# First stage of a graph layer on one Trainium2 core: 16-bit sort masks by whole groups, ScalarE's pair work a group later, weights prepared later

## What is computed

```
hx   = einsum('ni,rio->rno', x, weight)          # one product per relation
msg  = hx[edge_type, src]                        # one row per edge
agg  = segment_sum(msg, dst, num_segments=50000)
node = agg * 0.5**0.5 + h_bias + (x @ loop_weight) * 0.5**0.5
out  = layernorm(x + node, eps=1e-5)             # per row, no scale or shift
```

## Time and profile before

| | us |
|---|---|
| median of 3 runs | 802.35 (802.19 to 805.64) |
| profiled execution, its own time | 802.23 |
| its span in the trace | 800.5 |
| busy PE / PEld | 674.3 / 597.8 |
| busy DVE / ACT / POOL | 575.1 / 477.2 / 417.0 |

### The profile page before, as it was taken

How to read it: one execution, slowest core, us unless ns; L and a number is a source line. 1 busy time by engine, 2 the same in 40 slices (tenths; PEclk the granted TensorE clock), 3 DMA queues, 4 the chain that set the end, 5 groups by cost and what they waited for, 6 DMA issues and landing times. The chain is left out here.

```text
span 800.5 us, 16173 instructions
## 1 busy us (share of the span) xinstructions
PE 674.3 (84%) x4648; PEld 597.8 (75%) x4648; DVE 575.1 (72%) x2146; ACT 477.2 (60%) x1143; POOL 417.0 (52%) x426
## 2 busy tenths in 40 slices
PE   1658777768999999999999999999999999999720
PEld 1436656757999999999899999877887788788510
DVE  7906899965565665665565678888898898898830
ACT  2546680255556665556655566778777777777721
POOL 1000000426777777777777630376676676776463
PEclk9969999889999999999999999999999999999955
DMA  5301000656777776778777678988899999998621
GB/s 170 123 16 48 1 0 1 190 196 212 229 236 260 251 237 240 223 232 280 240 240 222 201 244 287 287 297 301 292 326 333 322 317 323 305 325 302 226 87 45
DMA packets 78903, 173.44 MB, mean 217 GB/s; under 512 B 25744, under 2 KB 41426, under 8 KB 78817
## 3 DMA queue, kind: packets, MB, share of 16 engines
q1 hardware_dynamic: 59233, 125.16, 46.4%
q0 software_dynamic: 19584, 47.23, 18.0%
HBM read 100.47 MB, written 78.20 MB: 223 GB/s over the span
## 5 line engine op out<-in xcount | busy, mean ns | idle before, releaser
L727 DVE TENSOR_TENSOR xt_low<-xt_ps,xt_high 128x512 fp32r<-128x512 f32 x241 | 164.9, 685 | 130.0 <-ACT xt_high L938 129.7
L1116 PE MATMUL y_ps<-w_high,xt_high 128*128 128x256 f32 x752 | 213.9, 284 | 0.0
L1116 PE MATMUL y_ps<-w_low,xt_high 128*128 128x256 f32 x752 | 213.6, 284 | 0.0
L1116 PE MATMUL y_ps<-w_high,xt_low 128*128 128x256 f32 x752 | 213.4, 284 | 0.0
L520 POOL DMA_INDIRECT gathered<-in_x,src_at x105 | 108.6, 1034 | 175.0 <-DVE edge_at L721 143.3
L938 ACT ACTIVATE xt_high<-xt_ps 128x512 fp32r<-128x512 f32 x241 | 141.9, 589 | 72.9 <-PE xt_ps L1084 71.1
L973 ACT ACTIVATE y_out<-y_ps,rstd 128x256 f32<-128x256 f32 x376 | 156.3, 470 | 13.4 <-DMA out_rows<-y_out 12.9
L1116 PEld LDWEIGHTS y_ps<-w_high,xt_low 128*128 128x128 f32 x752 | 144.2, 192 | 8.3
L549 POOL DMA_INDIRECT out_rows<-y_fix,fix_at x99 | 98.4, 994 | 96.0 <-ACT y_fix L1012 73.0
L1116 PEld LDWEIGHTS y_ps<-w_low,xt_high 128*128 128x128 f32 x752 | 144.8, 193 | 0.2
L1116 PEld LDWEIGHTS y_ps<-w_high,xt_high 128*128 128x128 f32 x752 | 144.2, 192 | 0.0
(11 more groups left out here) (155 smaller groups left out, 992.8 us busy)
## 6 DMA issues: line engine op xcount, KB each, us to landing
x_in<-in_x SPq DMA_DIRECT2D x97, 512.0 KB, 4.8
out_rows<-y_out SPq DMA_DIRECT2D x97, 512.0 KB
message_in<-message_rows SPq DMA_DIRECT2D x99, 128.0 KB, 5.0
keys<-padded_dst SPq DMA_DIRECT2D x13, 508.0 KB, 7.3
w_rel<-in_L_gnn_weight SPq DMA_DIRECT2D x1, 2048.0 KB, 14.0
gathered<-in_x,src_at POOLq DMA_INDIRECT x105
message_rows<-message_out,edge_at POOLq DMA_INDIRECT x105
y_fix<-out_rows,fix_at POOLq DMA_INDIRECT x99
```

Source lines behind the costliest of these rows:

```text
L727: nc.vector.tensor_tensor(xt_low[:, q % XT_RING, :], xt_ps[q % 2][:, :], xt_high[:, q % XT_RING, :].bitcast(F32), ALU.subtract).then_inc(l ...
L1116: return nc.tensor.matmul(to, xt[:, at_row:at_row + P], w, start=start, stop=stop)
```

## The change

1. `startup` gets a new order and a parameter `late`. TensorE (`late` = 0) does pair k - 2 in step k, ScalarE (`late` = 1) its part of pair k - 3. Sorts follow a written-out pace: sort s comes in the first step k with 2.5 + 4 s < 4.9 (k - 3), ahead of the pair; what is left comes behind step 13. So step 4 has sort 0, step 5 sort 1, step 6 sorts 2 and 3, step 7 sort 4, and so on; sorts 12 and 13 are left for the end.
2. The sort masks of a group are made by three `tensor_tensor` instructions in 16 bit in place of 21 `tensor_scalar` in float32: an equality of tile numbers (7 x 106), an equality of lanes (7 x 128), and the product of the first with three fields (7 x 3 x 106), which waits for the first by a semaphore, `tiles_marked`. To fit 16 bit exactly, source and edge number are cut into three fields (`src_low`, the high bits of the source with the low bits of the edge, `edge_high`), and the lists are put together again from the 318 sums in eight steps.
3. TensorE's sort matmuls have 16-bit operands and 318 columns.
4. VectorE builds five groups of lane masks ahead in place of four, and the preparation of the weights (with two constants, `ones_r` and the zeroing of `bias_rows`) moves from ahead of the position chain to behind the masks of group 1 and the lane masks of group 6.
5. Behind the last group the lists come first, then offsets, then the relation weights. The wait for the last flag group moves behind `low(8)` and `low(9)`.
6. Counts: `total` is no longer copied out; one instruction adds and converts from PSUM.

```diff
+        FIELDS = 3
+        lane_of = keys[:, :, :, :].rearrange("p a b d -> p (a b d)")[:, 0:GROUP * P].bitcast(F16).rearrange("p (c l) -> p c l", l=P)
+        tile_of = sort_space[:, 0:2 * GROUP * FIELDS * MTP].rearrange("p (c v m) -> p c v m", v=FIELDS, m=MTP)
+        one_tile = sort_space[:, 2 * GROUP * FIELDS * MTP:2 * GROUP * (FIELDS + 1) * MTP].rearrange("p (c m) -> p c m", m=MTP)
-        flag_ps, sorted_ps, misc_ps = y_ps[3][:, 0:COLS + 2], y_ps[4][:, 0:2 * MTP], y_ps[5]
+        flag_ps, sorted_ps, misc_ps = y_ps[3][:, 0:COLS + 2], y_ps[4][:, 0:FIELDS * MTP], y_ps[5]
...
-        def startup(step_f, step_s, step_m):
-
-            m = 0
-            for k in range(GROUPS + 4):
-                if k < GROUPS:
-                    step_f(k)
-                if 1 <= k <= HOLD:
-                    step_m(k - 1)
-                if k >= 4:
-                    step_s(k - 4)
+        def startup(step_f, step_s, step_m, late):
+
+            sorts = 0
+            for k in range(GROUPS):
+                step_f(k)
+                while sorts < GROUPS and 2.5 + 4 * sorts < 4.9 * (k - 3):
+                    step_s(sorts)
+                    sorts += 1
+                if 0 <= k - late - 2 < HOLD:
+                    step_m(k - late - 2)
+            for k in range(sorts, GROUPS):
+                step_s(k)
...
-            for k in range(4):
+            for k in range(5):
                 build_lanes(k)
-
-            dve.wait_ge(loop_in, 16)
...
             dve.wait_ge(counts_summed, 1)
-            link(nc.vector.tensor_copy(total[:, :], misc_ps[:, R:2 * R]))
-            link(nc.vector.tensor_scalar(tot_f[:, :], total[:, :], float(P - 1), None, ALU.add))
-            link(nc.vector.tensor_copy(tot_i[:, :], tot_f[:, :]))
+            link(nc.vector.tensor_scalar(tot_i[:, :], misc_ps[:, R:2 * R], float(P - 1), None, ALU.add))
...
             def build_sort(k):
-                if k >= 2:
-                    dve.wait_ge(group_sorted, k - 1)
-                for c, slot in group_columns(k):
-                    nc.vector.tensor_scalar(lane_of[:, slot, :], iota_f[:, :], lo_f[:, c:c + 1], None, ALU.is_equal)
-                    nc.vector.tensor_scalar(tile_of[:, slot, 0, :], iota_f[:, 0:MTP], hi_f[:, c:c + 1], src_f[:, c:c + 1], ALU.is_equal, ALU.mult)
-                    last = nc.vector.tensor_scalar(tile_of[:, slot, 1, :], iota_f[:, 0:MTP], hi_f[:, c:c + 1], e1_f[:, c:c + 1], ALU.is_equal, ALU.mult)
-                last.then_inc(masks_sorted, 1)
+                cols = slice(k * GROUP, (k + 1) * GROUP)
+                to = slice((k % 2) * GROUP, (k % 2 + 1) * GROUP)
+                wait(dve, group_sorted, k - 1)
+                nc.vector.tensor_tensor(one_tile[:, to, :], lane_iota[:, 0:MTP].unsqueeze(1).broadcast_to([P, GROUP, MTP]),
+                                        tile_h[:, cols].unsqueeze(2).broadcast_to([P, GROUP, MTP]), ALU.is_equal).then_inc(tiles_marked, 1)
+                nc.vector.tensor_tensor(lane_of[:, to, :], lane_iota[:, :].unsqueeze(1).broadcast_to([P, GROUP, P]),
+                                        lane_h[:, cols].unsqueeze(2).broadcast_to([P, GROUP, P]), ALU.is_equal)
+                dve.wait_ge(tiles_marked, k + 1)
+                nc.vector.tensor_tensor(tile_of[:, to, :, :], one_tile[:, to, :].unsqueeze(2).broadcast_to([P, GROUP, FIELDS, MTP]),
+                                        fields[:, cols, :].unsqueeze(3).broadcast_to([P, GROUP, FIELDS, MTP]), ALU.mult).then_inc(masks_sorted, 1)
...
             for k in range(GROUPS):
                 build_sort(k)
-                if k + 4 < GROUPS:
-                    build_lanes(k + 4)
+                if k + 5 < GROUPS:
+                    build_lanes(k + 5)
+                if k == 1:
+                    prepare_weights()
...
+            dve.wait_ge(group_sorted, GROUPS)
+            link(nc.vector.tensor_copy(found[:, :], sorted_ps))
...
+            nc.vector.tensor_tensor(src_at[:, :], found_high[:, :], found[:, 0:MTP], ALU.add).then_inc(list_ready, 1)
+            link(nc.vector.tensor_tensor(found_edge[:, :], found_edge[:, :], found_low[:, :], ALU.add))
+            link(nc.vector.tensor_scalar(empty[:, :], found_edge[:, :], 0.0, float(SKIP), ALU.is_equal, ALU.mult))
+            nc.vector.tensor_tensor(edge_at[:, :], found_edge[:, :], empty[:, :], ALU.add).then_inc(list_ready, 1)
...
-            dve.wait_ge(flag_grouped, GROUPS)
             for part in range(8):
...
             low(HOLD)
             low(HOLD + 1)
+            dve.wait_ge(flag_grouped, GROUPS)
...
-            startup(flag_group, lambda k: None, raw_move)
+            startup(flag_group, lambda k: None, raw_move, 1)
...
-            startup(flag_group, sort_group, first_pair)
+            startup(flag_group, sort_group, first_pair, 0)
```

More of the change, by code:

```diff
@@ L211, in scratch @@
             return a if dt == F32 else a.bitcast(dt)
[L213 to L214 removed]
+        rel_i, src_i, dst_i, pos_i, hi_i, lo_i, e1_i, node_i, node_hi_i, src_high, edge_low, edge_high, src_low = (scratch(EC, I32) for _ in range(13))
+        rel_f, pos_f, e1_f, dead, node_lo, node_hi = (scratch(EC) for _ in range(6))
+        lane_h, tile_h = (scratch(EC // 2).bitcast(F16) for _ in range(2))
+        fields = scratch(FIELDS * EC // 2).bitcast(F16).rearrange("p (c v) -> p c v", v=FIELDS)
         onehot, running, placed = (scratch(R * EC) for _ in range(3))
@@ L226, in gnn_layernorm_kernel @@
         rel_n = scratch(MTP)
-        empty = scratch(MTP)
+        found = running[:, 0:FIELDS * MTP].bitcast(I32)
+        found_high, found_edge, found_low, empty = (running[:, (FIELDS + i) * MTP:(FIELDS + 1 + i) * MTP].bitcast(I32) for i in range(4))
         key_i, next_i = (onehot[:, i * P:(i + 1) * P].bitcast(I32) for i in range(2))
@@ L254, in gnn_layernorm_kernel @@
         masks_sorted = sem("masks_sorted")
+        tiles_marked = sem("tiles_marked")
         group_sorted = sem("group_sorted")
@@ L617, in _ @@
             nc.vector.tensor_copy(column_f[:, :], column_i[:, :])
[L618 to L622, removed]
+            nc.vector.tensor_copy(e1_f[:, :], e1_i[:, :])
+            nc.vector.tensor_scalar(edge_low[:, :], e1_i[:, :], 15, 6, ALU.bitwise_and, ALU.logical_shift_left)
+            link(nc.vector.tensor_scalar(edge_high[:, :], e1_i[:, :], 4, None, ALU.logical_shift_right))
+            nc.vector.tensor_copy(fields[:, :, 2], edge_high[:, :])
+            nc.vector.tensor_scalar(dead[:, :], e1_f[:, :], E + 0.5, 512.0, ALU.is_gt, ALU.mult)
             dve.wait_ge(rel_in, 32)
@@ L639, in _ @@
             dve.wait_ge(nodes_ready, 2)
+            link(nc.vector.tensor_tensor_scan(running[:, :], onehot[:, :], onehot[:, :], 0.0, ALU.add, ALU.max))
+            nc.vector.tensor_copy(prior[:, 1:R], rn[:, 0:R - 1, EC - 1])
+            dve.wait_ge(src_in, 32)
+            nc.vector.tensor_scalar(src_low[:, :], src_i[:, :], 1023, None, ALU.bitwise_and)
+            link(nc.vector.tensor_scalar(src_high[:, :], src_i[:, :], 10, None, ALU.logical_shift_right))
+            nc.vector.tensor_copy(fields[:, :, 0], src_low[:, :])
+            nc.vector.tensor_tensor(fields[:, :, 1], src_high[:, :], edge_low[:, :], ALU.add)
             def build_lanes(k):
@@ new lines, in prepare_weights @@
+            def prepare_weights():
+                dve.wait_ge(loop_in, 16)
+                dve.wait_ge(bias_in, 16)
+                link(nc.vector.tensor_scalar(w_main[:, :], w_main[:, :], C, None, ALU.mult))
+                for k in range(KT):
+                    d = w_main[:, k * D + k * P:k * D + k * P + P]
+                    link(nc.vector.tensor_tensor(d, d, ident[:, :], ALU.add))
+                wm = w_main[:, :].rearrange("p (k n) -> p k n", k=KT)
+                nc.vector.tensor_reduce(w_mean[:, 0:KT], wm, AX_X, ALU.add)
+                link(nc.vector.tensor_reduce(w_mean[:, KT:KT + 1], bias_b[:, :], AX_X, ALU.add))
+                link(nc.vector.tensor_scalar(w_mean[:, 0:KT + 1], w_mean[:, 0:KT + 1], 1.0 / D, None, ALU.mult))
+                for k in range(KT):
+                    d = w_main[:, k * D:(k + 1) * D]
+                    nc.vector.tensor_scalar(d, d, w_mean[:, k:k + 1], None, ALU.subtract)
+                nc.vector.tensor_copy(bias_rows[:, :], zero[:, :])
+                nc.vector.tensor_copy(ones_r[:, :], ones[:, :])
+                link(nc.vector.tensor_scalar(bias_b[:, :], bias_b[:, :], w_mean[:, KT:KT + 1], None, ALU.subtract))
+                nc.vector.tensor_copy(bias_rows[0:1, :].rearrange("p (t d) -> p t d", t=2), bias_b[0:1, :].unsqueeze(1).broadcast_to([1, 2, D]))
+                nc.vector.tensor_copy(bias_high[:, :], bias_b[:, :])
+                link(nc.vector.tensor_copy(w_high[:, :], w_main[:, :]))
+                nc.vector.tensor_tensor(bias_rows[32:33, :].rearrange("p (t d) -> p t d", t=2), bias_b[32:33, :].unsqueeze(1).broadcast_to([1, 2, D]),
```

(2 more changed lines are left out.)

44 lines of the change are left out of this document (10 added, 34 removed).

## The result

| | before | after |
|---|---|---|
| median, us | 803.12 of 4 runs (802.19 to 805.64) | 779.06 of 4 runs (778.44 to 779.61) |
| span of the profiled execution | 800.5 | 777.2 |
| first transpose of the main loop | 147.22 | 123.07 |
| from there to the end of the span | 653.3 | 654.1 |
| VectorE's stops ahead of sort masks | 31.5 in 5 | 11.4 in 1 |

The ratio is 0.9695, with a 95% interval of 0.967 to 0.972. The forecast was 777, within 769 to 785.

What follows compares the result with a forecast made beforehand. The first stage, paced by VectorE's sort masks and its 31.5 us of stops, was taken as the bound. It would end at 122.4 instead of 147.2; 800.5 - 24.8 + 1.7 = 777.4 us, range 769 to 785.

Steps and rivals of the forecast that it cites:

- Masks: VectorE's three 16-bit mask instructions: 4.25 us a group in place of 4.82, at 1.04 ns an element.
- The tail: From VectorE's last masks to the end of the first stage: 11.6 us, costing 3.3 against the kernel before.
- The stop: VectorE idle for 10.6 us, about 41 to 52, until sort 0 is done, as TensorE waits for the late weights.
- the first pair: TensorE's pair 0, from 41.2 once the weights are ready: 3.8 us up to ScalarE's move.
- The clock: TensorE's granted clock: low for four or five us from near 41, then 1.00 to about 86.
- (b): Rival: TensorE stays at the low clock through the pairs, step 7.9 us; 781 to 796 us, chance 0.07.
- (a): Rival: VectorE's 16-bit masks stream at twice the rate, group 3.4 us with lane masks; 755 us, chance 0.08.
- (c): Rival: the repeated 16-bit operand streams slower than f32 on VectorE; at double, about 834 us; chance 0.03.
- (d): Rival: VectorE's stop moves and its four later stops (7.9 us) come back; 785 us, chance 0.03.
- first gather: POOL's gathers start at about 115 in place of 147.44; counted as no gain, at most a microsecond.
- The part behind the stage: From the main loop's first transpose to the end: moves as a block, 653 us as now.
- is the sum of both engines' work: First stage, old order: a step adds TensorE's and ScalarE's work, 10.33 us at low clock, 8.02 at high.

Runs made afterwards that it cites:

- e4: The changed kernel with the weights prepared early, right behind the five groups of lane masks, ahead of the position chain: 767.65 us, ratio 0.956.
- e1: The changed kernel with the old order of startup, all else as changed: 819.1 us, ratio 1.021.
- e3: The kernel before with the new order of startup alone, f32 masks and early weights: 774.76 us, ratio 0.964.
- e7: e4 with the group's seven columns innermost in the masks, so TensorE reads at a step of seven elements: 784.77 us, ratio 0.977.
- e9: e5 with every lane, tile and field value stored twice side by side, masks still contiguous for TensorE: 748.27 us, ratio 0.932.
- e5: e4 with the offsets of the relations ahead of VectorE's wait for the last sort: 765.04 us, ratio 0.952.
- e10: e9 with the sorts a step earlier in the written order: 744.90 us, ratio 0.928.
- e2: e1 with the weights prepared early, where they were before the change: 805.67 us of 10 runs, ratio 1.0035.
- e8: e2 with fourteen useless matmuls ahead of each sort group on TensorE: 804.24 us of 12 runs, ratio 1.000.

## Why the prediction held

**Stage by stage.** Masks: 4.25 forecast, 4.24 measured. The masks of sort 0 started at 24.2 as forecast, the weights were ready at 41.1 as forecast. The last masks ended at 111.3 (110.8), the stage at 123.07 (122.4), ScalarE's columns at 93.19 (93). Of the earlier trace rows's 138.9 this is 27.6 earlier: 20.1 from the stops and 8.3 from 14 groups at 0.59, less 0.8, most of which is the weights: 6.14 in their new place (34.95 to 41.09), 5.58 in the old one (15.98 to 21.56). The tail grew by 3.5 (3.3 forecast), which leaves 24.1 (24.8).

**The stop** was 11.4, not 10.6. The term that was too small is the first pair, 3.8 from the earlier trace rows up to ScalarE's move of it: from 41.14 to the move at 45.89 it took 4.75. The columns behind the move, and with them flag group 4 (50.13, forecast 49.3) and sort 0, are late by about the same 0.8. The pair's eight product matmuls took 3.38. The same ones took 2.06 in the kernel before (at 28.85), 2.15 in e4, 2.81 in e1 and 3.00 in e3, so a price from one row was good only to about a microsecond. Why they differ is open.

**The clock.** The forecast was the low level for four or five us from 41 on. The four transposes took 1.11 there and 0.60 at 46.87, as forecast, but the granted clock is given as 1.00 for all of 41 to 46. For these first microseconds the clock and the durations don't tell the same, and rival (b) is answered by the durations behind 46.87 and by 1.00 in 46 to 86.

**What VectorE waits for.** Rivals (a) and (c) fell with the 1.04 ns an element. Rival (a) had a true core: the same elements do run at 0.60 ns (e7: 0.89 us more for 1484 elements more) and faster in pairs (e9: 742 elements in 0.46, 896 in 0.54 from start to start, some 0.52 ns an element), once both operands advance along the innermost run. The Trainium skill's page "Vector Engine (DVE) Microarchitecture Reference", section "5.1 Performance modes — why throughput varies by op and dtype", drew this line: two sources of 2 bytes give two elements a cycle where every innermost step is 1 and every innermost run is longer than one element, and one element read again and again gives the plain rate. The rows agree on both sides of it: e9 runs at twice the rate of the change, e7 at 1.7 times. Rival (d) fell with the single stop.

**The end.** GpSimd's first gather came at 116.44, not about 115, since its lists were complete only at 115.4. The second took 5.25, beside VectorE's splits of the weights (117.43 to 122.25). But in e5, e9 and e10 three gathers beside the same splits took 1.3 to 1.5 each, so the splits alone do not explain it and the cause is open; TensorE did not wait for it. The part behind the stage took 654.1 in place of 653.3; over all twelve changed kernels here, whose stage ends between 89.3 and 163.6, it took 651.8 to 654.8. It does move as a block, to within 1.5 us.

**The step that was wrong** did not enter the forecast's sum. The prediction says that a step of the old order "is the sum of both engines' work", and rival (d) that "flag, pair and sort still chain through ScalarE". Flags and pair do; the sort does not: it lies beside ScalarE's 4.44 in a step of 8.02 that is 8.03 when the sort takes 1.12 in place of 2.67 (e2, 77.49 to 85.52). I built e1's and e2's expectations on it and missed both by 14. So the forecast came out right although this step was wrong, because in the new order VectorE is last and a step of the old order is not in the sum. Two more things are not in the prediction: the stops go by the order alone (e3), and the late weights, which it prices as the new stop of 10.6 but never sets against leaving them early, cost 11.4 of what the order gave.

## What to carry to other kernels

Before costing a shorter instruction, write down the loop of waits that sets the step and see whether it is in it: the same 16-bit masks, with their tail, cost 2.7 us with one order and gave 7.1 with the other. Of a change of several parts, run the parts alone; here masks and late weights together took time away, and the order alone beat the whole. When an operand is broadcast along the innermost dimension in 16 bit, store it twice and let the innermost run be two, and look at what the reader of the result does with the layout before turning it instead.

## What was not expected of the hardware

- A two-operand instruction in 16 bit took 1.04 ns an element with one operand repeated along the row, 0.60 with the group's seven columns innermost, and 742 elements took 0.46 from start to start (30.27 to 30.73) with runs of two.
- A 16-bit matmul of 318 columns took 0.136 us with contiguous operands (7 in 0.95) and 0.49 with both at a step of seven elements.
- One 128x512 subtraction on GpSimd took 18.7 us beside VectorE's two-operand masks, which were not slowed, and about 1.2 behind them, where VectorE's 0.21 us steps became 1.3.
- In the profiled run of e2, with the sort shortened and TensorE's pauses at 3.32 in place of 1.77, the granted clock of 63 to 96 was 0.90 in place of 1.00, and three of four steps took 9.7 us in place of 8.02; with useless matmuls in the pause, the profiled run of e8 had 1.00 and 8.02 again.
